# A mixture-of-experts block on one core: rewritten road to the first expert, later upper weight halves, last row group transposed behind six products

## Chip, core and metric

The kernel runs on one core of a Trainium2 chip. The metric is the device time of one execution in microseconds (us). The engines are TensorE (PE; its weight loads are listed as PEld), VectorE (DVE), ScalarE (ACT), GpSimd (POOL) and SyncE (SP). Each has its own instruction queue, and they wait for each other by semaphores only.

## What is computed

A transformer block on x of shape 2 x 2048 x 256: linear attention, then a mixture of 8 experts with 2 experts per token and a fixed capacity of 640 rows per expert. The change lies in the second half:

```python
logits = xf @ router_w.T
probs = jax.nn.softmax(logits, axis=-1)
topw, topi = jax.lax.top_k(probs, K)                       # K = 2
capacity = max(1, int(CF * N / E))                         # 640 of N = 4096 rows, E = 8
order = jnp.lexsort((-fw, fe))                             # by expert, then by falling weight
rank = jnp.arange(N * K) - starts[se]
keep = rank < capacity
disp = jnp.zeros((E, capacity + 1, D), x.dtype).at[se, pos].set(xf[st])
g = jnp.einsum('ecd,edf->ecf', disp, wg)
u = jnp.einsum('ecd,edf->ecf', disp, wu)
eo = jnp.einsum('ecf,efd->ecd', jax.nn.silu(g) * u, wd)    # D = 256, F = 1024
out = jnp.zeros_like(xf).at[st].add(contrib)
```

## The kernel before

**Stages.** All is written by hand in five queues. The attention stage walks 32 tiles of 128 tokens and writes normalised rows to the DRAM tensor `h_rows`. Then comes the road to the first expert, a chain with almost nothing beside it:

1. `choose` (L742) gives each token its two experts and weights `wgt`.
2. A search of 15 steps (L876 to L892) finds for each expert the bit pattern `cand` of the weight at the capacity limit. In each step DVE counts (`hit`, L880), PE sums the counts (L1272), and DVE picks the next pattern (L884 to L891). The 15 steps are a hardware loop of 3 turns of 5 steps.
3. `place_masks`, `place_counts`, `place_slots` (L899 to L939) turn "weight above / equal to the threshold" into a slot number for each token. They run in two parts, `PLACES = ((0, 2), (2, E))`: experts 0 and 1 first, the other six later. PE helps with four products against a triangular matrix `before` and a matrix of ones.
4. `describe(e)` (L973) splits the slot numbers of expert e into tile number (`tile_no`, `in_tile`) and row (`row_in`), makes `facts` (L962) and a one-hot matrix `onehot` (L970, four pieces), and PE's `look(e)` (L1288, 32 small products) reads off which token stands in each slot. `find_tokens` (L990) turns that into the index list `g_idx`.
5. POOL gathers the rows of expert e by five indirect DMAs of 128 rows (L496); PE transposes them (`transpose_x`, L1296) in row groups of 2, 2 and 1 tiles; ACT rounds them (`xT_h`, L634) and DVE makes the remainder (`xT_l`, L1027).

**Experts.** For each of 8 slices f of the hidden dimension, PE does `gate_up(f)` (24 products of 320 columns, 12 for each half h of the 640 rows, six for the gate and six for the up matrix), and then `down(f-1)` (15 products, L1341). ACT and DVE make `hid_h` and `hid_l` from it. In the shade of expert e the rows of expert e+1 are transposed at f = 4, 5, 6 (at 5, 6, 7 for the first expert), its weights are split into `w_h` (ACT, L625) and `w_l` (DVE, L1013), and `look(e+2)` runs at the end.

**Weights.** SP loads each expert's weights in a lower half (f 0 to 3, semaphore `raw_a`) and an upper half (f 4 to 7, `raw_b`), five DMAs and 1.5 MB each (L331). Both go into one buffer `w_raw`, so that a half is loaded as soon as the split of the expert before has read it: `expert` in the SP block (L394) waits for `sp_h` and `sp_l`.

## Time and profile before

| | |
|---|---|
| time, median of 3 runs | 678.95 us (678.22 to 679.12) |
| the profiled execution's own time | 678.13 us |
| its span in the trace | 676.0 us, 2.13 us less |
| PE busy | 568.7 us (84%) |
| DVE busy | 456.5 us (68%) |
| ACT / POOL busy | 320.0 / 269.0 us |
| chain that ended last | PE 59%, DVE 13%, issue 7% |
| mean DMA rate | 111 GB/s |

Spans and busy times come from one execution recorded by the hardware profiler. "Busy" for PE does not mean that it runs at its peak. In timeline rows the columns are start, length, engine, line, operation, output<-inputs, shapes, count, and in brackets the idle time before it with what ended it.

### The profile page before, as it was taken

The page shows a single profiled execution, that of the slowest core. Times are in us where ns is not written, and L with a number is a line of the kernel's source. Part 1 is how long each engine was busy: PE and PEld are TensorE (multiplying, and loading weights), DVE is VectorE, ACT ScalarE, POOL GpSimd, SP SyncE. Part 2 cuts the span into 40 slices and gives each one's busy share as a digit, 9 for nine tenths or more (in the row PEclk, how much of TensorE's full clock was granted, in tenths as well). Part 3 has the DMA queues.
Part 4 walks back from the last instruction along what each step waited for, and adds up shares of the span by engine and source line. Part 5 has one row for each costly group of instructions (what it writes and reads, how often), then busy time and mean ns, then how long its engine had stood idle before and what let it go on. Part 6 is the DMA issues. An engine that isn't in the chain of part 4 may idle for free.

```text
span 676.0 us, 13788 instructions
## 1 busy us (share of the span) xinstructions
PE 568.7 (84%) x4041; PEld 529.4 (78%) x4041; DVE 456.5 (68%) x1304; ACT 320.0 (47%) x717; POOL 269.0 (40%) x427
## 2 busy tenths in 40 slices
PE   4999889998997101279999999999999999999990
PEld 3577668887776000169999999999999999999990
DVE  3577889897677877867756766567667666666431
ACT  3688778886444500034534534445345444454330
POOL 5688757776678000302007025043070160442304
PEclk9999999999999555569989999999999999999996
DMA  5322268545554900144408317344174073340203
GB/s 164 94 64 78 71 194 264 189 145 162 157 190 153 264 0 0 40 133 133 133 1 213 94 44 170 95 141 102 61 198 106 18 194 95 110 102 9 32 1 39
DMA packets 91911, 75.24 MB, mean 111 GB/s; under 512 B 12108, under 2 KB 88278, under 8 KB 91864
## 3 DMA queue, kind: packets, MB, share of 16 engines
q1 hardware_dynamic: 82872, 58.77, 28.6%
q0 software_dynamic: 8992, 15.90, 11.2%
q8 instruction: 24, 0.39, 0.2%
q14 instruction: 23, 0.19, 0.1%
HBM read 52.48 MB, written 22.16 MB: 110 GB/s over the span
## 4 chain that ended last, share of the span: by engine, by line
PE 59%; DVE 13%; issue 7%; POOL 3%; ACT 2%; DMA 2%; DVEq 1%; SPq 0%; ACTq 0%; POOLq 0%
PE bank L1329 33%; PE bank L1341 15%; PE bank L1247 3%; PE bank L1292 2%; DVE hit L880 2%; PE bank L1150 2%; PE bank L1306 1%; DMA mod_all<-mod_store 1%; DVE x L847 1%; DVE st L849 1%; POOL out L506 1%; PE bank L1227 1%; PE bank L1236 1%; DMA xg<-h_rows,g_idx 1%; PE bank L1202 0%
## 5 line engine op out<-in xcount | busy, mean ns | idle before, releaser
L1329 PE MATMUL bank<-xT_h,w_h 128*128 128x320 f32 x512 | 160.2, 313 | 2.3 <-DVE xT_l L1027 1.7
L1329 PE MATMUL bank<-xT_l,w_h 128*128 128x320 f32 x512 | 159.2, 311 | 0.4 <-issue 0.4
L1329 PE MATMUL bank<-xT_h,w_l 128*128 128x320 f32 x512 | 159.0, 311 | 0.0
L496 POOL DMA_INDIRECT xg<-h_rows,g_idx x40 | 43.8, 1095 | 274.5 <-DVE g_idx L999 264.7
L1055 DVE TENSOR_TENSOR hid<-act_g,bank 128x320 f32<-128x320 f32 x128 | 62.0, 484 | 74.1 <-ACT act_g L648 59.6
L652 ACT CAST hid_h<-hid 128x320 fp32r<-128x320 f32 x128 | 58.9, 460 | 97.5 <-DVE hid L1055 92.8
L648 ACT ACTIVATE act_g<-bank 128x320 f32<-128x320 f32 x128 | 55.8, 436 | 103.3 <-PE bank L1329 96.2
L1329 PEld LDWEIGHTS bank<-xT_h,w_h 128*128 128x128 f32 x512 | 97.6, 191 | 3.0 <-DVE w_l L1013 2.1
L1329 PEld LDWEIGHTS bank<-xT_h,w_l 128*128 128x128 f32 x512 | 97.5, 190 | 0.5 <-issue 0.5
L1329 PEld LDWEIGHTS bank<-xT_l,w_h 128*128 128x128 f32 x512 | 97.5, 190 | 0.5 <-issue 0.5
L1341 PE MATMUL bank<-w_h,hid_h 128*128 128x256 f32 x320 | 91.4, 286 | 0.4 <-DVE hid_l L1060 0.4
L506 POOL DMA_INDIRECT out<-yo,s_idx x40 | 66.3, 1657 | 62.0 <-DVE yo L1045 50.7
L1060 DVE TENSOR_TENSOR hid_l<-hid,hid_h 128x320 fp32r<-128x320 f32 x128 | 62.8, 491 | 39.1 <-ACT hid_h L652 33.9
L1341 PE MATMUL bank<-w_h,hid_l 128*128 128x256 f32 x320 | 89.2, 279 | 0.0
L1341 PE MATMUL bank<-w_l,hid_h 128*128 128x256 f32 x320 | 89.0, 278 | 0.0
L1013 DVE TENSOR_TENSOR w_l<-w_raw,w_h 128x768 fp32r<-128x768 f32 x64 | 61.1, 960 | 7.9 <-ACT w_h L625 6.0
L1341 PEld LDWEIGHTS bank<-w_h,hid_h 128*128 128x128 f32 x320 | 60.2, 188 | 0.7 <-ACT hid_h L652 0.6
L1341 PEld LDWEIGHTS bank<-w_l,hid_h 128*128 128x128 f32 x320 | 60.5, 189 | 0.0
L1341 PEld LDWEIGHTS bank<-w_h,hid_l 128*128 128x128 f32 x320 | 60.3, 188 | 0.0
L1150 PE MATMUL bank<-wqkv_h,hT_h 128*128 128x256 f32 (+1 forms) x128 | 49.2, 384 | 6.0 <-DVE hT_l L819 4.7
L625 ACT CAST w_h<-w_raw 128x768 fp32r<-128x768 f32 x64 | 52.9, 833 | 0.0
L484 POOL TENSOR_TENSOR rot<-rot_a,rot_b 128x512 f32<-128x512 f32 x32 | 42.2, 1320 | 17.1 <-DVE rot_b L812 16.9
(180 smaller groups left out, 1118.2 us busy)
## 6 DMA issues: line engine op xcount, KB each, us to landing
w_raw<-wg SPq DMA_DIRECT2D x32, 256.0 KB, 3.3
w_raw<-wu SPq DMA_DIRECT2D x32, 256.0 KB, 4.4
w_raw<-wd SPq DMA_DIRECT2D x16, 512.0 KB, 6.1
x_in<-x SPq DMA_DIRECT2D x32, 128.0 KB, 2.1
q_store<-qT SPq DMA_DIRECT2D x32, 128.0 KB, 1.9
q_in<-q_store SPq DMA_DIRECT2D x32, 128.0 KB, 2.2
x_re<-x SPq DMA_DIRECT2D x32, 128.0 KB, 2.2
out<-x SPq DMA_DIRECT2D x32, 128.0 KB, 1.9
```

The lines of the kernel that those rows point to most:

```text
L484: nc.gpsimd.tensor_tensor(rot[s.par(0)][:, :], rot_a[:, :], rot_b[:, :], ALU.add).then_inc(rope_d, 1)
L496: nc.gpsimd.indirect_dma_start(out=xg[par][:, a, :], out_offset=None, in_=h2_rows, in_offset=bass.IndirectOffsetOnAxis(ap=g_idx[par][:, a: ...
L506: nc.gpsimd.indirect_dma_start(out=out_rows, out_offset=bass.IndirectOffsetOnAxis(ap=s_idx[par][:, a:a + 1], axis=0), in_=yo[:, a, :], in_ ...
L625: nc.scalar.copy(w_h[:, f, :], w_raw[:, f, :]).then_inc(sp_h, 1)
L648: nc.scalar.activation(act_g[h][:, :], bank[2 * h][:, 0:HCAP], ACT.Silu).then_inc(silu_d, 1)
L652: nc.scalar.copy(hid_h[f % 2][:, h * HCAP:(h + 1) * HCAP], hid[h][:, :]).then_inc(hh_d, 1)
L1013: V.tensor_tensor(w_l[:, f, :], w_raw[:, f, :], w_h[:, f, :].bitcast(F32), ALU.subtract).then_inc(sp_l, 1)
L1055: V.tensor_tensor(hid[h][:, :], act_g[h][:, :], bank[2 * h + 1][:, 0:HCAP], ALU.mult)\
L1060: V.tensor_tensor(hid_l[f % 2][:, h * HCAP:(h + 1) * HCAP], hid[h][:, :], hid_h[f % 2][:, h * HCAP:(h + 1) * HCAP].bitcast(F32), ALU.subtr ...
L1150: ins = MM(out, x[j][:, k, :], w[i][:, k, cols], start=n == 0, stop=n == 3 * KC - 1)
L1329: last = MM(bank[2 * h + m][:, 0:HCAP], W[i][:, f, at:at + P], XT[j][:, k, cols], start=n == 0, stop=n == 3 * KC - 1)
L1341: last = MM(bank[4 + a // 2][:, a % 2 * D:(a % 2 + 1) * D], (hid_h, hid_l)[j][f % 2][:, a * P:(a + 1) * P], (w_h, w_l)[i][:, f, 4 * P:], s ...
```

## The change

It does five things.

- The search is written out, 15 steps in a row, with no loop on DVE or PE.
- Slots are computed by a shorter formula. `before` now holds 0 above the diagonal and -1 elsewhere, so that PE delivers "rows before me minus all rows", and the running sum can be added directly. Slots are int32, tokens over the capacity just get a tile number of 5 or more, and tile numbers come from a shift by 7 bits. The first part covers expert 0 alone.
- The one-hot matrix is made in four pieces by token tile (the inner dimension) and no longer by row, and `look` waits piece by piece. `find_tokens` is one reduction.
- Row groups are (0, 1), (2,), (3, 4). The first half of the first `gate_up` waits for two groups only; the last group is transposed after its first six products, into bank 7.
- SP loads the upper weight half of expert e+1 only when the first row group of expert e+1 has been transposed (`trx_d`).

```diff
-XG = -(-CT // 2)
+ROW_GROUPS = ((0, 1), (2,), (3, 4))
+XG = len(ROW_GROUPS)
-PLACES = ((0, 2), (2, E))
+PLACES = ((0, 1), (1, E))
...
                 wait(sp, sp_h, e * FC + FC)
                 wait(sp, sp_l, e * FC + FC)
+                wait(sp, trx_d, (e + 1) * XG + 1)
                 load_weights(e + 1, FC // 2, raw_b)
...
-            nc.gpsimd.affine_select(out=before[:, :], in_=ones_b[:, :], compare_op=ALU.is_gt, fill=0.0, base=0,
+            nc.gpsimd.affine_select(out=before[:, :], in_=zeros_b[:, :], compare_op=ALU.is_gt, fill=-1.0, base=0,
                                     pattern=[[1, P]], channel_multiplier=-1).then_inc(plink_s, 1)
...
-                        .then_inc(ga_d[a // 2], 16)
+                        .then_inc(ga_d[next(g for g, t in enumerate(ROW_GROUPS) if a in t)], 16)
...
-            with dve.Fori(0, DIGITS // SEARCH) as i:
-                for j in range(SEARCH):
-                    n = i * SEARCH + j
...
+            for n in range(DIGITS):
...
-                V.tensor_scalar(need[:, lo:hi], run[:, 0, lo:hi, NT - 1], -1.0, float(CAP), ALU.mult, ALU.add)
-                for k in range(2):
-                    ins = TT(flat(pre[:, k, lo:hi, :]), flat(run[:, k, lo:hi, :]), tot[k], ALU.subtract)
-                link(ins)
-                for k in range(2):
-                    ins = TT(flat(pre[:, k, lo:hi, :]), flat(pre[:, k, lo:hi, :]), rows[k], ALU.add)
-                ins.then_inc(pre_d, 1)
+                V.tensor_scalar(above[:, lo:hi], run[:, 0, lo:hi, NT - 1], 1.0, None, ALU.add)
+                V.scalar_tensor_tensor(flat(pre[:, 0, lo:hi, :]), flat(run[:, 0, lo:hi, :]), 1.0, rel[0], ALU.add, ALU.add)
+                TT(flat(pre[:, 1, lo:hi, :]), flat(run[:, 1, lo:hi, :]), rel[1], ALU.add).then_inc(pre_d, 1)
...
-                TT(t, pre[:, 1, lo:hi, :], need_b, ALU.is_lt)
-                link(TT(at, pre[:, 1, lo:hi, :], need_b, ALU.min))
-                link(TT(t, t, mask2[:, 1, lo:hi, :], ALU.mult))
-                TT(kept, t, mask2[:, 0, lo:hi, :], ALU.add)
-                link(TT(at, at, pre[:, 0, lo:hi, :], ALU.add))
-                link(V.scalar_tensor_tensor(kept, at, float(CAP), kept, ALU.is_lt, ALU.mult))
-                link(V.scalar_tensor_tensor(at, at, 1.0, kept, ALU.add, ALU.mult))
-                link(V.tensor_scalar(at, at, -1.0, None, ALU.add))
+                link(TT(p1, p1, above_b, ALU.add))
+                TT(p0, p0, mask2[:, 0, lo:hi, :], ALU.mult)
+                link(TT(p1, p1, mask2[:, 1, lo:hi, :], ALU.mult))
+                link(V.scalar_tensor_tensor(slot[:, lo:hi, :], p0, -1.0, p1, ALU.add, ALU.add))
...
-                TT(tile_ge[:, :, :], sl.unsqueeze(2).to_broadcast([P, NT, CT + 1]),
-                   tile_thr[:, :].unsqueeze(1).to_broadcast([P, NT, CT + 1]), ALU.is_ge).then_inc(ge_d, 1)
-                dve.wait_ge(ge_d, e + 1)
-                RED(tile_no[:, :], tile_ge[:, :, 1:], AX, ALU.add).then_inc(tn_d, 1)
-                TT(in_tile[:, :, :], tile_ge[:, :, 0:CT], tile_ge[:, :, 1:], ALU.subtract).then_inc(in_d, 1)
+                V.tensor_scalar(tile_no[:, :], sl, TILE_BITS, None, ALU.arith_shift_right).then_inc(tn_d, 1)
                 dve.wait_ge(tn_d, e + 1)
+                TT(in_tile[:, :, :], tile_no[:, :].unsqueeze(2).to_broadcast([P, NT, CT]),
+                   tile_id[:, :].unsqueeze(1).to_broadcast([P, NT, CT]), ALU.is_equal).then_inc(in_d, 1)
...
-                sl = slice(part * P // 4, (part + 1) * P // 4)
-                TT(onehot[:, sl, :], iota_b[:, sl, :], row_in[:, :].unsqueeze(1).to_broadcast([P, P // 4, NT]),
+                sl = slice(part * NT // 4, (part + 1) * NT // 4)
+                TT(onehot[:, :, sl], iota_b[:, :, sl], row_in[:, sl].unsqueeze(1).to_broadcast([P, P, NT // 4]),
                    ALU.is_equal).then_inc(facts_d, 1)
...
-                V.tensor_copy(got[:, :, :], bank[7][:, 0:NV * CT].rearrange("p (v a) -> p v a", v=NV))\
-                    .then_inc(got_d, 1)
-                dve.wait_ge(got_d, e + 1)
-                lk(V.scalar_tensor_tensor(tok[:, :], got[:, 1, :], float(P), got[:, 0, :], ALU.mult, ALU.add))
-                lk(V.tensor_scalar(tok[:, :], tok[:, :], -float(P), 0.0, ALU.add, ALU.max))
-                V.tensor_copy(g_idx[par][:, :], tok[:, :]).then_inc(idx_d, 1)
+                    RED(g_idx[par][:, :], bank[7][:, 0:NV * CT].rearrange("p (v a) -> p a v", v=NV), AX, ALU.add)\
+                        .then_inc(idx_d, 1)
...
-            x_low(0, 0, 0, bk=0)
             place_slots(1)
+            x_low(0, 0, 0, bk=0)
             x_low(0, 0, 1, bk=1)
             split_low(0, 4, 4)
-            x_low(0, 0, 2, bk=2)
+            x_low(0, 0, 2, bk=7)
...
-                wait(pe, facts_d, e * 4 + 4)
                 for n in range(NT):
+                    if n % (NT // 4) == 0:
+                        wait(pe, facts_d, e * 4 + n // (NT // 4) + 1)
...
-            for g in range(XG):
+            for g in range(XG - 1):
                 transpose_x(0, 0, g, first=True)
...
-                if f == 0:
-                    wait(pe, xl_d, e * XG + XG)
                 for h in range(2):
+                    if f == 0:
+                        wait(pe, xl_d, e * XG + XG - 1 + h)
...
+                        if first and (h, m) == (0, 0):
+                            transpose_x(0, 0, XG - 1, first=True)
```

**DVE, from the counts to the tile numbers of expert 0.** Before, the eight slot operations (L932 to L939) and the four of `describe_tiles` read:

```order
L932 TENSOR_TENSOR tmp_s<-pre,need 128x64 [waits pre_d]
L933 TENSOR_TENSOR slot<-pre,need 128x64
L934 TENSOR_TENSOR tmp_s<-tmp_s,mask 128x64 [waits link_s]
L935 TENSOR_TENSOR keep<-tmp_s,mask 128x64 [waits link_s]
L936 TENSOR_TENSOR slot<-slot,pre 128x64
L937 SCALAR_TENSOR_TENSOR keep<-slot,keep 128x64 [waits link_s]
L938 SCALAR_TENSOR_TENSOR slot<-slot,keep 128x64 [waits link_s]
L939 TENSOR_SCALAR slot<-slot 128x64 [waits link_s]
L948 TENSOR_TENSOR tile_ge<-slot,tile_thr 128x192 [waits iota_d,link_s]
L951 TENSOR_REDUCE tile_no<-tile_ge 128x32 [waits ge_d]
L952 TENSOR_TENSOR in_tile<-tile_ge 128x160
L954 SCALAR_TENSOR_TENSOR row_in<-tile_no,slot 128x32 [waits tn_d]
```

Now the same stretch is:

```order
L924 TENSOR_TENSOR pre<-pre,above 128x32 [waits pre_d]
L925 TENSOR_TENSOR pre<-pre,mask 128x32 [waits link_s]
L926 TENSOR_TENSOR pre<-pre,mask 128x32
L927 SCALAR_TENSOR_TENSOR slot<-pre 128x32 [waits link_s]
L936 TENSOR_SCALAR tile_no<-slot 128x32 [waits iota_d,link_s]
L938 TENSOR_TENSOR in_tile<-tile_no,tile_id 128x160 [waits tn_d]
L940 SCALAR_TENSOR_TENSOR row_in<-tile_no,slot 128x32
```

Twelve instructions with nine waits have become seven with five, on 32 instead of 64 elements in the slot part.

**PE, from the first rows of expert 0 to its first products.** L1306 is a transposition (two for each tile and group), L1329 a product of `gate_up`. Before:

```order
L1306 MATMUL bank<-const_sb,xg 128x128 [waits ga_d0]
L1306 MATMUL bank<-const_sb,xg 128x128 x3
L1306 MATMUL bank<-const_sb,xg 128x128 [waits ga_d1]
L1306 MATMUL bank<-const_sb,xg 128x128 x3
L1306 MATMUL bank<-const_sb,xg 128x128 [waits ga_d2]
L1306 MATMUL bank<-const_sb,xg 128x128
L1329 MATMUL bank<-xT_h,w_h 128x320 [waits xl_d,sp_l]
```

Now (L1278 is the transposition, L1301 the product):

```order
L1278 MATMUL bank<-const_sb,xg 128x128 [waits ga_d0]
L1278 MATMUL bank<-const_sb,xg 128x128 x3
L1278 MATMUL bank<-const_sb,xg 128x128 [waits ga_d1]
L1278 MATMUL bank<-const_sb,xg 128x128
L1301 MATMUL bank<-xT_h,w_h 128x320 [waits xl_d,sp_l]
L1301 MATMUL bank<-xT_l,w_h 128x320
L1301 MATMUL bank<-xT_h,w_l 128x320
L1301 MATMUL bank<-xT_h,w_h 128x320
L1301 MATMUL bank<-xT_l,w_h 128x320
L1301 MATMUL bank<-xT_h,w_l 128x320
L1278 MATMUL bank<-const_sb,xg 128x128 [waits ga_d2]
L1278 MATMUL bank<-const_sb,xg 128x128 x3
```

The last group, now two tiles and four transpositions, stands behind six products, and the six products wait for two groups only.

**SP, head of the loop over experts.** L331 (now L327) loads the upper half of the next expert. Before:

```order
L405 UNCONDITIONAL_BRANCH
L405 ISA
L331 ISA [waits sp_l,sp_h]
L331 DMA w_raw<-wg 128x4x128
L331 ISA
L331 DMA w_raw<-wg 128x4x128
L331 DMA w_raw<-wu 128x4x128 x2
L331 ISA
L331 DMA w_raw<-wd 128x4x256
```

Now:

```order
L402 UNCONDITIONAL_BRANCH
L402 ISA
L75 ISA [waits sp_l,sp_h]
L327 ISA [waits trx_d]
L327 DMA w_raw<-wg 128x4x128
L327 ISA
L327 DMA w_raw<-wg 128x4x128
L327 DMA w_raw<-wu 128x4x128 x2
L327 ISA
L327 DMA w_raw<-wd 128x4x256
```

A wait for `trx_d` stands ahead of the first of the five DMAs; the load of the lower half of the expert after it follows in the same queue.

## Rows read from the trace of the kernel before

**Rows 1.** Stretch, length; busy PE, PEld, DVE, ACT, POOL; clock, DMA share, GB/s

```profile
298.20:339.90 41.70, 41.23 (x325) 40.92 (x323) 31.56 (x68) 20.56 (x42) 5.21 (x5) 1.00 0.38 113
```

**Rows 2.** Timeline of DVE, steps of the search (the first count of each step)

```profile
232.68 0.48 DVE L880 TENSOR_SCALAR_CACHE_REDUCE hit<-valT,cand 128x256 bf16<-128x256 f32 x1 [0.22 <-DVE valT L875]
...
234.92 0.48 DVE L880 TENSOR_SCALAR_CACHE_REDUCE hit<-valT,cand 128x256 bf16<-128x256 f32 x1
...
241.65 0.48 DVE L880 TENSOR_SCALAR_CACHE_REDUCE hit<-valT,cand 128x256 bf16<-128x256 f32 x1
...
244.38 0.48 DVE L880 TENSOR_SCALAR_CACHE_REDUCE hit<-valT,cand 128x256 bf16<-128x256 f32 x1 [0.52 <-DVE cand L891]
...
267.48 0.23 DVE L894 TENSOR_SCALAR thr_sel<-const_sb,cand 128x8 f32<-128x8 f32 x1 [0.21 <-DVE cand L891]
```

**Rows 3.** Timeline of DVE from the masks to the index list of expert 0

```profile
268.61 0.73 DVE L904 TENSOR_TENSOR mask<-wgt,thr_b 128x64 bf16<-128x64 f32 x2
...
270.32 0.17 DVE L918 TENSOR_SCALAR need<-run 128x2 f32<-128x2 f32 x1
...
271.16 0.23 DVE L932 TENSOR_TENSOR tmp_s<-pre,need 128x64 f32<-128x64 f32 x1
...
272.96 0.36 DVE L948 TENSOR_TENSOR tile_ge<-slot,tile_thr 128x192 f32<-128x192 f32 x1
...
273.94 0.56 DVE L962 TENSOR_TENSOR facts<-vals,in_tile 128x160 bf16<-128x160 bf16 x2
274.42 2.49 DVE L970 TENSOR_TENSOR onehot<-iota_b,row_in 128x1024 bf16<-128x1024 bf16 x4
279.11 0.17 DVE L994 COPY got<-bank 128x10 f32<-128x10 f32 x1 [2.21 <-PE bank L1292]
...
279.72 0.17 DVE L999 CAST g_idx<-tok 128x5 int32<-128x5 f32 x1
279.80 1.85 DVE L904 TENSOR_TENSOR mask<-wgt,thr_b 128x192 bf16<-128x192 f32 x2
```

**Rows 4.** Timeline of PE, the look of expert 0

```profile
276.96 2.11 PE L1292 MATMUL bank<-facts,onehot 128*128 128x10 bf16 x32 [7.17 <-DVE onehot L970]
```

**Rows 5.** Timeline of POOL, gathers of row tiles 2 and 3 of expert 0

```profile
284.44 1.41 POOL L496 DMA_INDIRECT xg<-h_rows,g_idx  x1 [0.30 <-issue]
286.15 0.94 POOL L496 DMA_INDIRECT xg<-h_rows,g_idx  x1 [0.30 <-issue]
```

**Rows 6.** Timeline of PE, second and last row group, first product of expert 0

```profile
289.68 1.11 PE L1306 MATMUL bank<-const_sb,xg 128*128 128x128 f32 x4 [2.13 <-DMA xg<-h_rows,g_idx]
291.22 0.69 PE L1306 MATMUL bank<-const_sb,xg 128*128 128x128 f32 x2 [0.43 <-DMA xg<-h_rows,g_idx]
293.64 0.60 PE L1329 MATMUL bank<-xT_h,w_h 128*128 128x320 f32 x1 [1.72 <-DVE xT_l L1027]
```

**Rows 7.** Timeline of DVE, remainder of the first row group

```profile
288.21 0.69 DVE L1027 TENSOR_TENSOR xT_l<-bank,xT_h 128x512 fp32r<-128x512 f32 x1 [0.89 <-ACT xT_h L634]
```

**Rows 8.** Busy time in chosen stretches, from the first product on

```profile
293.64:298.20 4.56, 4.56 (x17) 4.56 (x18) 0.52 (x2) 0.44 (x2) 0.00 (x0) 0.50 0.96 280
...
339.90:346.10 6.20, 6.20 (x50) 6.20 (x51) 1.45 (x2) 0.53 (x3) 0.00 (x0) 0.72 0.01 3
...
359.52:364.23 4.71, 3.97 (x27) 3.62 (x26) 1.94 (x3) 1.72 (x4) 4.07 (x3) 1.00 0.91 292
```

**Rows 9.** Chain that ended last: start, length, what; 24 undisturbed products

```profile
366.00 3.52 PE bank L1329 x24
```

**Rows 10.** Timeline of SP, first loads of a lower weight half

```profile
330.02 0.93 SPq L331 DMA_DIRECT2D w_raw<-wg  x2
```

**Rows 11.** Busy time in a stretch at the end of those loads

```profile
338.00:340.00 2.00, 1.53 (x15) 1.34 (x14) 1.31 (x3) 1.46 (x3) 0.00 (x0) 1.00 0.00 0
```

**Rows 12.** Timeline of ACT, first split of an upper half, then the next silu

```profile
333.68 0.84 ACT L625 CAST w_h<-w_raw 128x768 fp32r<-128x768 f32 x1
335.77 0.44 ACT L648 ACTIVATE act_g<-bank 128x320 f32<-128x320 f32 x1 [1.25 <-PE bank L1329]
```

More of the change, by code:

```diff
@@ L1268, in _ @@
             last.then_inc(r_pe, 1)
[L1269 to L1272 removed]
+            for n in range(DIGITS):
+                pe.wait_ge(cnt_d, n + 1)
+                MM(bank[1][:, 0:3], same_e[:, :], cnt[:, :], start=True, stop=True).then_inc(tot_d, 1)
             pe.wait_ge(r_dve, 3)
```

91 lines of the change are left out of this document (38 added, 53 removed).

## The prediction

> **What bounds the kernel now.** I read the busy time by stretch first, then the timelines of the stretch in which PE is idle. From 298.2 to 339.9 us PE is busy 41.23 of 41.70 us at full clock [rows 1], and the stretches after it look alike: in the experts the bound is PE, and what other engines save there is worth nothing. Ahead of them stands the road. From the first count of the search at 232.68 us [rows 2] to the first product of expert 0 at 293.64 us [rows 6] there are 61 us in which each step waits for the one before it, mostly on DVE. A microsecond saved on that chain is a microsecond of the kernel, until the rows of expert 0 are gathered. After that three transpositions, ACT and DVE stand between the last gather and the first product.
>
> **The search, written out.** The first counts of two neighbouring steps stand 2.24 us apart; across the turn of the loop it is 241.65 to 244.38, 2.73 us [rows 2]. So a turn costs 0.49 us. Two turns give 0.98 us. The idle time before the first step is 0.22 us and before `thr_sel` 0.21 us, where waits elsewhere on the road leave 0.03 us: 0.19 and 0.18 us more. Sum: 1.35 us. The bound below is nothing, if straight code is fetched too slowly; the attention stage is partly straight code too, and no row there shows it, so I take 1.35. The Trainium skill (Advanced Engine Details and Errata, Control Flow Timing) gives about 108 ns for a compare-and-branch. Two turns would then be an estimated 0.22 us, and this trace doesn't agree: its turn takes 0.49 us.
>
> **Masks, counts, slots, tiles.** Two masks take 0.73 us at 64 elements and 1.85 us at 192 [rows 3], 4.4 ns an element, so 0.45 us at 32: 0.3 saved. From `need` at 270.32 to `tmp_s` at 271.16 are 0.84 us for two subtractions, a wait and two additions; now one small operation and two additions without a wait between them, about 0.42; with shorter scans ahead of them (an estimated 0.1) the saving is 0.5. Slots: 271.16 to 272.96, 1.80 us for eight operations of which each waited one costs some 0.23. Now three waited ones and one that overlaps, 0.76: 1.05 saved. Tiles: 272.96 to 273.94, 0.98 us; now a shift (about 0.2) and a comparison of 160 elements (0.36 at 192), 0.56: 0.4 saved.
>
> **The look.** The one-hot matrix takes 2.49 us in four pieces, and PE begins at 276.96 when all are there and is read at 279.11 [rows 3, 4]: 2.15 us. Now PE works behind each piece. A quarter of the look (about 0.5 us) is shorter than a piece (0.62), so after the last piece only a quarter and the pipe remain, 0.65 us: 1.5 saved. The open cost is the one-hot itself: its inner run shrinks from 32 to 8 elements. No row shows such a pattern. Below, it costs nothing (0.62 us a piece); above, it falls to the rate of the remainder operation, 0.69 us for 512 elements [rows 7], that is about 1.3 us a piece and 2.8 us in all. It is nearest to today's row (same types, same count, still neighbours in memory), so I take nothing. The Trainium skill (VectorE: DVE Perf Modes, What auto-detection actually checks) has 16-bit tensors with step 1 run two elements a cycle, which also speaks for no change; the trace's 0.62 us for 1024 elements agrees for the long run only.
>
> **Tokens.** 279.11 to 279.89 (279.72 + 0.17) becomes one operation of some 0.17 [rows 3]: 0.6 saved.
>
> Up to the index list: 1.35 + 0.3 + 0.5 + 1.05 + 0.4 + 1.5 + 0.6 = **5.7 us**.
>
> **The first products.** I keep the clock of the old trace, counted from the index list. POOL's issue for tile 3 ends at 287.09 and its rows free PE at 289.68, 2.6 us later; tile 2's issue ends at 285.85 [rows 5], so its rows are there by 288.45. Then the transposition of one tile (0.69 [rows 6]), ACT (0.4) and DVE (0.4, both estimates, half of 0.69 and a hand-over) and 0.15: first product at 290.2 in place of 293.64. DVE could be later than that, because `place_slots(1)` now stands ahead of the first remainder (288.21 before [rows 7]). Before, DVE was free at 287.32, 0.89 us ahead of that remainder. Masks of seven experts add 0.3, scans 0.15, the four slot operations 1.55, and the counts give back 0.4 (estimates from the rows above, scaled to 224 elements): 288.9, and with two remainders (0.69 and 0.4) 290.0. So it just fits. The start gains 3.4 us. The last group is landed at 291.2 [rows 6] and PE comes to it after six products at 0.27 us, at 291.9: no wait. Its four transpositions (1.1 us) now lie inside the products. But at half clock the product rate is half too: 17 products in 4.56 us at 0.50 [rows 8], so if the clock rises as long after the start as before, they displace about four products which run later at full clock, 24 in 3.52 us [rows 9]: 0.6 us. Net **2.8 us**. ACT's table load now follows the last rounding and ends about 0.4 us after the first half is ready; PE has the second half to do meanwhile.
>
> **Upper weight halves.** In expert 1 one `gate_up` takes 4.71 us, with gathers, scatters and the upper half of expert 2 at 292 GB/s beside it [rows 8], and 3.52 us undisturbed [rows 9]. PE waits there for no semaphore. The load goes to a time after most of the scatters: **1.0 us** of the 1.19, since its new place has some traffic as well. Does it come late? Five such DMAs are issued from 330.02 on and no byte moves after 338.0 [rows 10, 11], 8 us at most. In expert 0 the first group of expert 1 is transposed at f = 5, one slice before that of f = 6. A slice is an estimated 5.7 us: 24 products 3.52 [rows 9], the 15 of `down` at 256 columns by the same rate 1.76, transpositions 0.4 to 0.5. ACT rounds the f = 6 group just before 333.68, so the one of f = 5 is transposed at about 326.5, and the half is there at 334.5 at the latest. ACT wants it at 333.68 and has until 335.77 [rows 12] for 0.84 us of work: no delay of PE. In later experts it is issued at f = 4 and wanted at f = 6, some 13 us later. Behind it in SP's queue stands only the next lower half, wanted 15 us on.
>
> **Sum.** 5.7 + 2.8 + 1.0 = 9.5 us. The profiled execution took 678.13 us, so 668.6; it lies 0.8 below the median of the runs, so I predict **669.4 us** as a median.
>
> **Rivals.**
> - *The dip of the clock after expert 0 disappears.* From 339.9 to 346.1 the granted clock is 0.72 on average [rows 8]: PE does a look there, with its 10-column products, and then runs for a while at 1.2 in place of 2.4 GHz; (1 - 0.72) of 6.2 us is 1.7 us. The last remainder ahead of this look now has two tiles, not one, and everything is shifted in time. If the clock holds, 667.7 us. 0.15.
> - *The one-hot in short runs goes at the slow rate.* Plus 2.8: 672.2 us. 0.10.
> - *The early start is eaten.* DVE's longer queue ahead of the first remainder, or the last rows landing late while PE stands before them in order. The 2.8 us are lost, and the traffic stall only moves to another place: 673.2 us. 0.10.
> - *Upper halves come late, slower than before.* ACT would wait in `split_high` at f = 6 in seven experts, behind it the next silu. To turn 9.5 us of gain into over 1.4 us of loss each would have to cost 1.6 us, so with 13 us of cover and about 3 us that PE can spare, a load would have to take 17 us or more; it takes 8. 0.03: about 681.
> - *The road is shorter but the kernel isn't*, because gathers wait for stores into `h_rows`: these were issued long before. 0.02: 678.
>
> **How the numbers follow.** My forecast has 0.60. A measurement of this kernel tells 0.2% (1.4 us) from no change. Faster by more than that: 0.60 + 0.15 + 0.10 + 0.10 = 0.95. The range goes from 665.8 (clock dip gone and 2 us more on the road, where most terms are estimates) to 673.2, which takes in the slow one-hot and the eaten start.
>
> **What the profile would show.** Steps of the search 2.24 us apart throughout; 5.7 us less from its first count to POOL's first gather; one-hot pieces of 0.6 us (1.3 if the rival holds); PE's transpositions of the last group after six products with no DMA wait ahead; first product some 9.1 us earlier than at 293.64; all `gate_up` of expert 1 at 3.5 us; ACT's `w_h` of f = 4 never waiting long on DMA. The prediction fails if PE waits anew between 285 and 300 us, or in every expert at f = 6.

## The result

Median of before 679.12 us (678.22 to 681.04), of the changed kernel **673.86 us** (671.94 to 675.32), five runs each: a ratio of 0.9922, 95% interval 0.9902 to 0.9942. The gain is 5.3 us; forecast were 9.5 us, and the time lies 0.7 us above the range. Both sides of the balance were off: the road gained more than forecast, and the experts behind it gave some 6 us back. (In the two profiles the spans differ by only 2.9 us, 676.0 to 673.1, because in the changed kernel's the search also happens to start 1.4 us later, at 234.09 in place of 232.68.)

**The road.** DVE in the changed kernel, two neighbouring steps of the search, its end, and the way to the index list (answers to [rows 2, 3]):

```profile
234.09 0.48 DVE L876 TENSOR_SCALAR_CACHE_REDUCE hit<-valT,cand 128x256 bf16<-128x256 f32 x1
...
236.24 0.48 DVE L876 TENSOR_SCALAR_CACHE_REDUCE hit<-valT,cand 128x256 bf16<-128x256 f32 x1
...
266.39 0.23 DVE L890 TENSOR_SCALAR thr_sel<-const_sb,cand 128x8 f32<-128x8 f32 x1
...
270.80 2.49 DVE L956 TENSOR_TENSOR onehot<-iota_b,row_in 128x1024 bf16<-128x1024 bf16 x4
274.00 0.17 DVE L970 TENSOR_REDUCE g_idx<-bank 128x5 int32<-128x10 f32 x1 [0.72 <-PE bank L1264]
```

Steps are 2.15 us apart, not 2.24, and from the first count to `thr_sel` it is 32.30 us in place of 34.80. The one-hot in runs of 8 costs what it did in runs of 32: 2.49 us. The index list stands 39.91 us after the first count, before 47.04.

PE in the changed kernel, the first products (answers to [rows 4, 6]):

```profile
271.54 2.43 PE L1264 MATMUL bank<-facts,onehot 128*128 128x10 bf16 x32 [3.36 <-DVE onehot L956]
...
282.71 0.69 PE L1278 MATMUL bank<-const_sb,xg 128*128 128x128 f32 x2 [0.48 <-DMA xg<-h_rows,g_idx]
284.41 0.61 PE L1301 MATMUL bank<-xT_h,w_h 128*128 128x320 f32 x1 [1.01 <-DVE xT_l L999]
...
286.15 1.05 PE L1278 MATMUL bank<-const_sb,xg 128*128 128x128 f32 x4
```

The look starts behind the first one-hot piece; the last group is transposed after six products with no DMA wait ahead of it. From the first count to the first product: 60.96 us before, 50.32 now, a gain of 10.6 us (forecast 9.1).

**What was given back.** From the first product to the end of the span it was 676.0 - 293.64 = 382.4 us; it is 673.1 - 284.41 = 388.7. By the looks these 6.3 us fall apart as follows: expert 0, from its first product to the look at its end, takes 47.7 us in place of 46.3; expert 1, to the next look, 46.7 in place of 48.1; the next four experts together 186.8 in place of 182.1; the rest 107.5 in place of 105.9. The forecast had 0.6 us more for expert 0 (the transpositions that now stand behind its first product), 1.0 us less for expert 1, and nothing for the others. So experts 0 and 1 together cost nothing more, and the whole loss is in the experts after them.

The first place at which something changed is expert 0. SP in the changed kernel, the loads of the upper weight half of expert 1 and behind them the first of the next lower half (answers to [rows 10]):

```profile
317.97 0.95 SPq L327 DMA_DIRECT2D w_raw<-wg  x2
319.01 1.77 SPq L327 DMA_DIRECT2D w_raw<-wu  x2
320.98 0.37 SPq L327 DMA_DIRECT2D w_raw<-wd  x1
321.68 1.21 SPq L327 DMA_DIRECT2D w_raw<-wg  x2
```

ACT in the changed kernel, the split that waits for that half (answers to [rows 12]):

```profile
324.46 0.37 ACT L632 CAST xT_h<-bank 128x256 fp32r<-128x256 f32 x1
326.69 0.83 ACT L623 CAST w_h<-w_raw 128x768 fp32r<-128x768 f32 x1 [1.86 <-DMA w_raw<-wd]
```

PE in the changed kernel, the look behind it:

```profile
332.09 2.04 PE L1264 MATMUL bank<-facts,onehot 128*128 128x10 bf16 x32 [1.31 <-DVE xT_l L999]
```

The half is issued at 317.97, and the lower half of expert 2 starts right behind it at 321.68. Its last part lands at 326.7, 8.7 us after the first issue; ACT stood for it for 1.86 us. Behind ACT's split stand two silus and the last rounding, behind these the last remainder on DVE, behind it the look: PE is idle 1.31 us (0.47 before). TensorE's clock behind this look is the same in both profiles. Busy time in the 8.95 us from the look on (columns as in [rows 1]: the granted clock is the third figure from the end), in the changed kernel:

```profile
332.09:341.04 8.95, 8.95 (x74) 8.95 (x75) 2.72 (x6) 1.34 (x3) 0.00 (x0) 0.81 0.01 2
```

In the kernel before:

```profile
339.90:348.85 8.95, 8.95 (x72) 8.95 (x73) 2.37 (x5) 1.42 (x4) 0.00 (x0) 0.81 0.01 2
```

The second place is every later expert. Their looks are 46.7 us apart on average (four intervals from 378.80 to 565.63), before 45.5 (387.97 to 570.08). PE in the changed kernel, the last product of f = 2 in expert 3:

```profile
441.67 0.31 PE L1301 MATMUL bank<-xT_h,w_l 128*128 128x320 f32 x1
```

ACT in the changed kernel, the silus around it:

```profile
440.25 0.44 ACT L646 ACTIVATE act_g<-bank 128x320 f32<-128x320 f32 x1 [0.94 <-PE bank L1301]
444.74 0.44 ACT L646 ACTIVATE act_g<-bank 128x320 f32<-128x320 f32 x1 [2.96 <-remote]
449.20 0.44 ACT L646 ACTIVATE act_g<-bank 128x320 f32<-128x320 f32 x1 [2.26 <-PE bank L1301]
```

The last product of f = 2 starts at 441.67 and is over by 442.0. ACT has nothing else to do, and its silu starts at 444.74. PE's signal came 2.7 us late: the profile has an update of the semaphore that ACT waits for just before 444.74, but no instruction that ended then, and calls that "remote". So it is the signal that is late, and not ACT that stands. The next one came late too (449.20; its products were done at 445.5), and PE then waited for `hid`. The kernel before shows the second of these, not the first, and had enough time to spare that it cost little, some 0.2 us an expert (45.5 us, against 45.3 in e17 below, the same kernel without a late signal).

POOL in the changed kernel, the first gather and the first scatter beside these silus:

```profile
437.63 1.02 POOL L494 DMA_INDIRECT xg<-h_rows,g_idx  x1 [31.31 <-DVE g_idx L970]
...
444.04 1.62 POOL L504 DMA_INDIRECT out<-yo,s_idx  x1 [0.30 <-issue]
```

The late signal was due 4.3 us after the first gather began, and 2 us before the first scatter stands in the trace.

### The profile page after: what moved, and what is told of

Its sections match the earlier page's. It is cut to its first block, busy times and chain, and to the rows that moved or that the text cites. A ratio compares the mean times of both kernels' runs of the same rounds, so it can differ in the third digit from the quotient of the medians.

```text
span 673.1 us, 13689 instructions
## 1 busy us (share of the span) xinstructions
PE 575.1 (85%) x4041; PEld 533.3 (79%) x4041; DVE 448.5 (67%) x1260; ACT 320.1 (48%) x717; POOL 263.6 (39%) x428
## 4 chain that ended last, share of the span: by engine, by line
PE 61%; DVE 12%; issue 5%; POOL 3%; DMA 2%; ACT 2%; another core or an unknown queue 1%; SPq 1%; DVEq 0%; ACTq 0%; POOLq 0%
PE bank L1301 33%; PE bank L1315 14%; DVE hit L876 3%; PE bank L1219 3%; PE bank L1122 2%; PE bank L1264 2%; PE bank L1278 1%; DVE x L845 1%; PE bank L1199 1%; DVE st L847 1%; DMA w_raw<-wd 1%; POOL out L504 1%; PE bank L1208 1%; DMA x_in<-x 1%
## 5 line engine op out<-in xcount | busy, mean ns | idle before, releaser
L1301 PE MATMUL bank<-xT_h,w_h 128*128 128x320 f32 x512 | 160.8, 314 | 4.6 <-DVE hid L1027 2.8
L1301 PE MATMUL bank<-xT_l,w_h 128*128 128x320 f32 x512 | 158.7, 310 | 0.0
L1301 PE MATMUL bank<-xT_h,w_l 128*128 128x320 f32 x512 | 158.7, 310 | 0.0
L494 POOL DMA_INDIRECT xg<-h_rows,g_idx x40 | 40.8, 1020 | 270.1 <-DVE g_idx L970 260.3
L1301 PEld LDWEIGHTS bank<-xT_h,w_h 128*128 128x128 f32 x512 | 97.4, 190 | 6.9 <-issue 4.9
L1301 PEld LDWEIGHTS bank<-xT_l,w_h 128*128 128x128 f32 x512 | 97.3, 190 | 0.1
L1301 PEld LDWEIGHTS bank<-xT_h,w_l 128*128 128x128 f32 x512 | 97.0, 189 | 0.0
L504 POOL DMA_INDIRECT out<-yo,s_idx x40 | 63.8, 1596 | 66.8 <-DVE yo L1017 55.5
L623 ACT CAST w_h<-w_raw 128x768 fp32r<-128x768 f32 x64 | 52.9, 834 | 1.9 <-DMA w_raw<-wd 1.9
```

The costliest lines, as they stand in the source:

```text
L494: nc.gpsimd.indirect_dma_start(out=xg[par][:, a, :], out_offset=None, in_=h2_rows, in_offset=bass.IndirectOffsetOnAxis(ap=g_idx[par][:, a: ...
L504: nc.gpsimd.indirect_dma_start(out=out_rows, out_offset=bass.IndirectOffsetOnAxis(ap=s_idx[par][:, a:a + 1], axis=0), in_=yo[:, a, :], in_ ...
L623: nc.scalar.copy(w_h[:, f, :], w_raw[:, f, :]).then_inc(sp_h, 1)
L1301: last = MM(bank[2 * h + m][:, 0:HCAP], W[i][:, f, at:at + P], XT[j][:, k, cols], start=n == 0, stop=n == 3 * KC - 1)
```

## The experiments

The experiments came to stand on four chips, which I number 2 to 5; the chip of the result above I count as chip 1, though the record doesn't name it. The kernel before, run beside each, took 679.1 us on chip 1, 681.5 on 2, 681.1 on 3, 675.7 on 4 and 674.7 to 675.4 on 5. This turned out to be part of the answer. Each chip was used in one stretch of time, so "chip" below can't be told apart from the hour. Each median is over 4 to 12 executions, 5 for the changed kernel on chip 1. "Road" is from the first count to the first product, "expert" the mean of the four intervals between looks from the end of expert 1 on.

| run | chip | median us | ratio (95%) | road | expert |
|---|---|---|---|---|---|
| changed kernel | 1 | 673.86 | 0.9922 (0.9902 to 0.9942) | 50.3 | 46.7 |
| e1_load_early | 2 | 679.38 | 0.9968 (0.9949 to 0.9987) | 50.4 | 47.4 |
| e2_before_load_late | 2 | 679.64 | 0.9972 (0.9955 to 0.9989) | 61.2 | 45.5 |
| e3_search_looped | 2 | 678.97 | 0.9962 (0.9945 to 0.9979) | 52.9 | 46.8 |
| e4_before_unrolled | 2 | 677.87 | 0.9955 (0.9936 to 0.9974) | 58.7 | 46.3 |
| e5_changed_again | 3 | 677.82 | 0.9953 (0.9940 to 0.9966) | 50.3 | 47.1 |
| e6_gather_later | 3 | 680.26 | 0.9989 (0.9967 to 1.0011) | 50.4 | 46.8 |
| e7_scatter_later | 3 | 666.89 | 0.9801 (0.9787 to 0.9815) | 50.4 | 45.4 |
| e8_before_one_op | 3 | 687.51 | 1.0102 (1.0078 to 1.0126) | 60.6 | 47.7 |
| e9_scatter_first | 4 | 670.63 | 0.9931 (0.9907 to 0.9955) | 50.3 | 46.0 |
| e10_before_scatter_later | 4 | 674.90 | 0.9994 (0.9981 to 1.0007) | 61.2 | 45.2 |
| e11_scatter_later_load_early | 4 | 665.88 | 0.9864 (0.9846 to 0.9881) | 50.5 | 45.3 |
| e12_scatter_same_time | 4 | 667.40 | 0.9876 (0.9859 to 0.9893) | 50.4 | 45.3 |
| e13_wait_long_true | 5 | 667.13 | 0.9877 (0.9853 to 0.9900) | 50.5 | 45.3 |
| e14_wait_for_dve | 5 | 668.01 | 0.9888 (0.9865 to 0.9911) | 50.4 | 45.4 |
| e15_changed_third | 5 | 668.31 | 0.9896 (0.9874 to 0.9919) | 50.4 | 45.4 |
| e16_wait_and_load_early | 5 | 666.23 | 0.9870 (0.9847 to 0.9893) | 50.4 | 45.4 |
| e17_before_itself | 5 | 675.49 | 0.9997 (0.9984 to 1.0009) | 61.2 | 45.3 |
| e18_scatter_same_time_again | 5 | 666.91 | 0.9874 (0.9851 to 0.9897) | 50.4 | 45.4 |

### The late load and the search, each undone and each alone (chip 2)

e1 takes this line out of the changed kernel, e2 adds it to the kernel before:

```diff
+                wait(sp, trx_d, (e + 1) * XG + 1)
                 load_weights(e + 1, FC // 2, raw_b)
```

e3 puts the loop of the search back in the changed kernel, e4 writes it out in the kernel before:

```diff
-            with dve.Fori(0, DIGITS // SEARCH) as i:
-                for j in range(SEARCH):
+            for n in range(DIGITS):
...
-            with pe.Fori(0, DIGITS // SEARCH) as i:
-                for j in range(SEARCH):
+            for n in range(DIGITS):
```

> The changed kernel, with only the moved upper weight halves put back to where they were (SP no longer waits for the transposition of the next rows). Theory A, the moved load is what ate the gain: after the first product the changed kernel took 388.7 us against 382.4, and the load stands in both of the places I found (in expert 0 ACT waited 1.9 us for it, with a late remainder, a late look and the low clock behind that; in each later expert PE lost some 1.3 us more between look and f = 4, where the load used to run). Then this version is about 6 us faster than the changed kernel: ratio to the kernel before about 0.984, 668 us, looks of later experts 45.5 us apart, no DMA wait of ACT near 326. Theory B, the loss per expert comes from something else that changed (other row groups, the look, code): only expert 0's part comes back (2 us) and the stall in expert 1 returns (1 us): ratio 0.990 or above, looks still 46.8 us apart.

> The kernel before, with only the moved upper weight halves added (one wait of SP). Theory A: slower than before by the same 5 to 6 us, ratio about 1.008, looks 46.8 us apart. Theory B: no more than the 1 us gain in expert 1 against some loss in expert 0: ratio 0.998 to 1.003, looks 45.5 us apart.

> The changed kernel with the search of 15 steps as a loop of 3 turns again, everything else as changed. By the steps of the two traces (34.80 against 32.30 us from the first count to thr_sel) writing it out gave 2.5 us, so this version is 2.5 us slower than the changed kernel, ratio to before about 0.996. Rival: the longer straight code costs something later (code to be brought in for DVE and PE, other places of the loops in memory): then the back end is shorter by some us and the ratio is near 0.992 or below.

> The kernel before with only the search written out. By the two traces 2.5 us faster: ratio 0.9963. My own prediction's sum has 1.35 us for it: 0.9980. Rival as in the run before: 1.0 or above if the longer code costs later what it gives in the search.

My theory fell. With the load put back, the experts take 47.4 us, not 45.5: the silu of f = 2, second half, comes 20.7 us after the look (19.2 in e3 with the load late, 16.4 where it should be). So the moved load doesn't make PE's signals late; on this chip it went with a smaller lateness. And with the load late in the kernel before, nothing is lost per expert, and the kernel is 0.28% faster, 1.9 us, an interval that leaves out 1. In the changed kernel the late load was worth more on this chip: e1 stands at 0.9968 and e3 at 0.9962 although e3's search is 2.5 us longer, which makes some 2.9 us.

These runs also test the price that the prediction gave the late load. It was read from one product stage of expert 1, f = 3, 4.71 us in place of 3.52 [rows 8]. The same stage in e2, where the half is issued 11.8 us after the start of the stage:

```profile
360.23:365.44 5.21, 4.28 (x26) 3.64 (x25) 1.47 (x3) 1.20 (x2) 4.30 (x4) 1.00 0.67 143
```

And in e17, the kernel before on chip 5, with the half loaded at its old time (issued from 357.69 on):

```profile
360.51:364.02 3.51, 3.51 (x26) 3.51 (x25) 2.26 (x5) 1.55 (x3) 2.90 (x3) 1.00 0.85 276
```

With the load moved away the stage stayed long; with the load beside it, on chip 5, the stage was short.

The search written out is worth 2.5 us in every run: from the first count to `thr_sel` 34.8 us in e2, e3, e8, e10, e17 and 32.3 us in all others. As a whole e4 gains 0.45%, or 3.1 us. Its experts take 46.3 us in the profile, though no edit stands behind the search; a signal of f = 3 comes 0.7 us later than in the kernel before on chip 1. Whether that is the edit or the chip isn't known, since the kernel before wasn't profiled on chip 2. The medians there leave e4 a gain no smaller than what its search saved, which speaks for the chip.

### When gathers and scatters are issued (chip 3)

e6 puts a clearing of a spare tile ahead of the gathers; e7 holds the scatters back; e8 gives the kernel before the index list in one operation (and the multiplied tile numbers that it needs):

```diff
+                wait_apart(pool, pz, e, apart)
+                nc.gpsimd.memset(idle_p[:, :], 0.0).then_inc(pz, 1)   # e6 alone
                 gather(e + 1, 1 - par)
+                wait_apart(pool, trx_d, (e + 1) * XG + 1, apart)      # e7 alone
                 scatter(e - 1, 1 - par)
```

> The changed kernel itself once more, on the chip of the next three runs, so that these have something to stand against. All theories: 0.992, looks of the experts 46.8 us apart.

> The changed kernel, with a clearing of a spare tile on POOL (some 0.6 us) ahead of the gathers in the loop of experts 1 to 6. What is found so far: in every expert, some 4.5 us after POOL's first gather, PE's signals to ACT come late by 2 to 4 us; PE does not stop by itself, but it has only about 1.5 us to spare until it needs what follows. In the kernel before the gathers start 12.6 us after the look and one signal is caught (that of f = 3, first half); in the changed kernel they start at 12.0 us and the signal ahead of it (f = 2, second half) is caught too. Theory P, phase: the shorter way from the look to the index list moved the gathers 0.6 us forward and into this signal. Then this version puts them back and the experts take 45.5 to 46 us: 5 to 8 us faster than the changed kernel, ratio about 0.983. Rival Q: the stall comes from something else that changed (the waits in the look, the row groups, the length of the code) and not from the time of the gathers: then the experts still take 46.8 us, ratio 0.992.

> The changed kernel, with POOL's scatters of the loop held back until the first group of the next rows is transposed (f = 4), some 9 us later than now. Theory G, the gathers alone make PE's signals late: the stall stays where it is (silu of f = 2, second half, 19.1 us after the look) at least at its start, and the time with it: ratio 0.99 or a little under, or above if scatters meet the weight loads. Theory S, the scatters (whose first starts 18.4 us after the look, shortly before the late signals come) make them late: the experts take 45.4 us up to there and any new stall stands 9 us later; ratio 0.983.

> The kernel before, with only the index list made by one operation instead of four, so that the gathers start 0.6 us earlier in every expert (and on the road to the first). Theory P, phase: the signal of f = 2, second half, is now caught here too, the experts take 46.5 us or more instead of 45.5, and the version is slower than before by 5 us: 1.008. Rival Q: only the 0.6 us on the road: 0.999, experts 45.5 us.

e6 didn't do what it was made for. POOL in e6, in expert 3:

```profile
441.38 0.53 POOL L525 MEMSET idle_p<- 128x512 f32 x1 [30.87 <-DVE g_idx L975]
442.14 1.03 POOL L496 DMA_INDIRECT xg<-h_rows,g_idx  x1 [0.23 <-issue]
```

The first gather of an expert starts about 1 us after the index list anyway (440.96 on DVE here), and the clearing fits into that time: the gathers moved by 0.1 us. It says nothing on the phase, and its higher time comes with more time at low clock in expert 1 (granted clock 0.61 from 331.35 to 340.00 and again 0.83 from 352 to 362 us).

e8 is the test of the phase (the time of the gathers within an expert) that worked. Its gathers start 12.0 us after the look (12.6 before), the silu of f = 2, second half, comes at 20.7 instead of 16.4 (the latter on chips 1 and 2), and saving 0.6 us on the road made the kernel 1.0% slower.

e7 is the other end. ACT in e5 in expert 4, the silus of f = 2 and of f = 3, first half:

```profile
484.80 0.44 ACT L646 ACTIVATE act_g<-bank 128x320 f32<-128x320 f32 x1 [0.93 <-PE bank L1301]
489.38 0.44 ACT L646 ACTIVATE act_g<-bank 128x320 f32<-128x320 f32 x1 [3.06 <-remote]
493.90 0.44 ACT L646 ACTIVATE act_g<-bank 128x320 f32<-128x320 f32 x1 [2.34 <-PE bank L1301]
```

The same three silus in e7:

```profile
482.49 0.44 ACT L647 ACTIVATE act_g<-bank 128x320 f32<-128x320 f32 x1 [0.94 <-PE bank L1302]
484.25 0.44 ACT L647 ACTIVATE act_g<-bank 128x320 f32<-128x320 f32 x1 [0.23 <-PE bank L1302]
487.78 0.44 ACT L647 ACTIVATE act_g<-bank 128x320 f32<-128x320 f32 x1 [1.33 <-PE bank L1302]
```

In e7 each silu follows its products at once, also at f = 4 to 6 where the scatters now are, beside the weight loads. The same chip, the same minutes, one wait of POOL: 677.82 to 666.89 us. With the lateness gone the gain over the kernel before is 14.2 us by medians, more than the 9.5 forecast, since the kernel before has late signals to lose as well.

e7 does two things at once: it moves the scatters by some 10 us, and it makes POOL wait between gathers and scatters. Which of the two cures isn't shown. That the signal of f = 2 was due before the first scatter stands in the trace (441.98 against 444.04 in the changed kernel) speaks against the plain reading that a scatter under way holds it up.

### Order, place, and waits (chips 4 and 5)

e9 swaps the two calls. e10 holds the scatters back in the kernel before, e11 is e7 without SP's wait. e12 to e14 put one wait between gathers and scatters that moves neither; e16 is e12 without SP's wait; e15 and e17 are the two kernels unchanged, e18 is e12 again:

```diff
                 gather(e + 1, 1 - par)
+                wait_apart(pool, gu_d, e * 2 * FC + 5, apart)    # e12, e16, e18
+                wait_apart(pool, idx_d, e + 2, apart)            # e13
+                wait_apart(pool, hid_d, e * 2 * FC + 5, apart)   # e14
                 scatter(e - 1, 1 - par)
```

> The changed kernel, with the scatters of the last rows ahead of the gathers of the next in POOL's loop, back to back as now. Holding the scatters back to f = 4 took away every late signal of PE (experts 45.4 us, kernel 0.980). Theory O, order: late signals come when scatters are issued right behind gathers whose rows are still on their way; with the order turned round they are small or gone, experts 45.3 to 45.8 us, ratio 0.981 to 0.984. Theory R, run: ten such DMAs back to back make them late in either order: experts 46.5 us or more, ratio 0.990 or above. The gathers then begin 21.5 us after the look and their first group is wanted at 27: if that is too late, PE waits there for rows, which the trace would show as a DMA wait ahead of the transpositions.

> The kernel before, with only the scatters of the loop held back until the first group of the next rows is transposed. Before, one signal came late by 2.3 us and cost PE next to nothing (0.1 us an expert). If the late signals are what the scatters cost, this gives 0.1 to 0.2 us in each of six experts, 1 us in all, and 1 us in expert 1, where a product stage stood at 4.71: ratio 0.997. If scatters next to weight loads cost anything by themselves, 1.0 or above.

> The changed kernel with the scatters held back, but with the upper weight halves where they were before (SP doesn't wait for the transposition). This isolates what the late load is worth when no signal comes late. If its only good was that it took traffic from the time of gathers and scatters, it is worth nothing now, and in expert 0 it costs (ACT waited 1.9 us for the half there): this version is 0.5 to 1.5 us faster than the one with scatters held back, ratio 0.978 to 0.980. If the load at f = 2 slows gathers or PE's signals even without scatters: experts over 45.4 us, ratio 0.983.

> The changed kernel with a wait of POOL between gathers and scatters that is over before the gathers are all issued (first product half of f = 2), so that the scatters start at the same time as now. A control: the late signal of f = 2, second half, is due 2 us before the first scatter stands in the trace. If it is the time of the scatters, nothing changes: experts 47 us, ratio 0.995. If POOL without a wait runs ahead of what the trace shows, and it is the waiting as such that helped, the signal of f = 2 comes in time (silu 16.4 us after the look in place of 19.1) and the ratio is 0.985 to 0.99.

e12 had its silu in time and experts of 45.3 us. I took that for a cure by a mere wait, and made three runs to find out which kind of wait:

> The changed kernel with a wait of POOL between gathers and scatters for something that has been true since before the gathers (the index list), so that POOL is never held, but the same instructions stand there as in the run that waited for the first half of f = 2. Theory N, an instruction in between is enough: silu of f = 2, second half, 16.4 us after the look, experts 45.3 us, about 8 us faster than the changed kernel. Theory H, POOL's queue has to be held: everything as in the changed kernel, silu at 19.1 us, experts 47 us.

> The same, with POOL waiting for DVE's product of f = 2, first half, which comes some 1 us after PE's signal that was waited for before. Theory H, held by whom doesn't matter: experts 45.3 us. Theory E, it is the wait for a signal of PE that brings PE's signals out in time: experts 47 us, silu at 19.1 us.

> The changed kernel again, on the chip of these runs. Experts 47 us, ratio 0.992 to 0.996.

> The changed kernel with the wait for PE's first half of f = 2 between gathers and scatters, and without the late load of the upper weight halves. With scatters held back to f = 4 the early load was 0.0012 of the kernel faster than the late one stood on another chip. Here traffic of gathers, scatters and weights falls together again at f = 2 to 4. If only PE's late signals made that dear: experts 45.3 us, expert 0 0.7 us shorter, ratio 0.001 to 0.002 under that of the late load. If the traffic itself is dear: experts 46 us or more.

The control e15 undid it. The changed kernel itself, with no wait of POOL, has no late signal on this chip: experts 45.4 us, 668.3 us in all. So e13 and e14 stood where there was nothing to cure, and e12 most likely too: the changed kernel wasn't run on chip 4, but the kernel before took there what it takes on chip 5 (675.7 and 674.7 to 675.4 us).

> The kernel before, unchanged, for its profile on this chip. If signals of PE come late here: before at 679 to 682 us, silu of f = 3, first half, 22.3 us after the look. If not: 674 to 676 us, that silu at 19.8 us, experts 45.2 us (as the version with scatters held back had them). The ratio should be 1.000 within 0.002.

> The changed kernel with POOL's wait between gathers and scatters that moves neither, once more. On a chip with late signals: if the wait does nothing, experts 47 us and a ratio of 0.992 to 0.996; if it cures them, experts 45.4 us and 0.980. On a chip without them it tells nothing new: 45.4 us, 0.988.

e17 agrees: the kernel before on chip 5 has its silu of f = 3, first half, at 19.9 us after the look, on chip 1 at 22.3. e18 stood on chip 5 again, so whether such a wait does anything where signals are late isn't known. e9 gains less than e12 on its chip, 0.9931 against 0.9876: its gathers start 22.1 us after the look, and the rows come too late for the first transposition: from the start of the products ahead of it to the transposition it is 4.24 us in place of 3.52, and PE waited for DMA in five experts, 0.25 to 0.59 us each, 2.35 us in all. e10 (0.9994) shows that holding the scatters back is worth nothing in the kernel before on chip 4.

Chip 5 has both kernels without late signals, and shows the late load without them. ACT in e15 (late load), the split of expert 0 that waits:

```profile
325.66 0.83 ACT L623 CAST w_h<-w_raw 128x768 fp32r<-128x768 f32 x1 [2.32 <-DMA w_raw<-wd]
```

PE in e15, the look behind it:

```profile
331.05 2.10 PE L1264 MATMUL bank<-facts,onehot 128*128 128x10 bf16 x31 [1.77 <-DVE xT_l L999]
```

The same split on ACT in e16 (early load):

```profile
322.20 0.84 ACT L623 CAST w_h<-w_raw 128x768 fp32r<-128x768 f32 x1
```

The same look on PE in e16:

```profile
328.81 2.20 PE L1264 MATMUL bank<-facts,onehot 128*128 128x10 bf16 x32 [0.55 <-DVE xT_l L999]
```

And busy time in the 8.95 us from that look on, in e15:

```profile
331.05:340.00 8.95, 8.95 (x62) 8.95 (x63) 1.44 (x2) 1.30 (x3) 0.00 (x0) 0.62 0.01 2
```

In e16:

```profile
328.81:337.76 8.95, 8.95 (x82) 8.95 (x83) 3.81 (x9) 2.01 (x5) 0.00 (x0) 1.00 0.01 2
```

In e17, the kernel before:

```profile
341.32:350.27 8.95, 8.95 (x73) 8.95 (x74) 2.51 (x5) 1.43 (x4) 0.00 (x0) 0.81 0.01 2
```

The late load delays the look (PE idle 1.77 us in place of 0.55). In this pair of profiles the clock behind the look differs too: it falls to 0.62 on average in e15, with 62 matmul records in the stretch, and not at all in e16, with 82. Expert 0 from its first product to this look: 48.4 us in e15, 46.8 in e16, 46.0 before. From this look to the next: 47.9, 45.3, 46.5. By these profiles the late load costs 4.4 us.

But these two profiles are the ends of the range. In the twenty profiles of this study PE idles 0.47 to 0.55 us ahead of this look with the early load, and the granted clock in the 8.95 us from it is 0.81 five times and 1.00 three times. With the late load PE idles 0.76 us in e2 and 1.16 to 2.32 us in the versions of the changed kernel, and the clock is 0.81 five times, the changed kernel on chips 1 and 3 among them, and 0.62 seven times. So the late load goes with a lower clock, but the idle time alone doesn't decide it: e13 idles 1.99 us and has 0.81, e7 idles 1.50 us and has 0.62.

By medians e15 and e16 are 2.1 us apart, and e12 and e11 on chip 4 1.5 us, with overlapping intervals; and each of these pairs differs by a second edit, POOL's wait. The pair that differs by the late load alone is e18 and e16, 0.9874 and 0.9870: 0.3 us. What the late load costs where no signal is late isn't shown beyond the idle time of PE; it lies between nothing and some 2 us.

## Why the prediction was wrong

The step that failed is the one that gave the experts a fixed time: "in the experts the bound is PE, and what other engines save there is worth nothing". The sum had nothing for them; the profile has 6.3 us, all of it behind expert 1. The term for the upper weight halves failed as well, in its cause. Term by term:

**Up to the index list, 5.7 us.** Right in kind, too small: 7.1 us (47.04 to 39.91). The search is the term: 1.35 us forecast, 2.5 measured. I priced the turns and the waits around the loop, and took the step of 2.24 us for granted. But a step written out takes 2.15 us: DVE's idle time ahead of `beats` fell from 0.30 to 0.21 us. The Trainium skill (Advanced Engine Details and Errata, Control Flow Timing) gives about 108 ns for a compare-and-branch. The loop here cost far more than its branches by that figure: 2.5 us over two turns and 15 steps. The other terms give 4.6 us together for 4.35 forecast.

**First products, 3.4 us earlier from the index list on.** Right: 3.5 (10.64 - 7.13). DVE reached the first remainder in time, and "no wait" ahead of the last group came out.

**Upper weight halves, "1.0 us" gained and "no delay of PE".** The reasons of this step failed, and its size on chip 1 came out by luck. The price came from the stage of 4.71 us, which I put down to the traffic of the half beside it. In e17 the same stage takes 3.51 us with 276 GB/s beside it, in e2 it takes 5.21 with the half moved away. Such long stages of expert 1 stand in profiles with late signals (before, e1, e2, e4, e8, 4.7 to 6.0 us) and in none of those from chip 5. ACT in the kernel before, the silus at the start and at the end of the long stage:

```profile
359.60 0.44 ACT L648 ACTIVATE act_g<-bank 128x320 f32<-128x320 f32 x1 [2.04 <-remote]
...
364.15 0.44 ACT L648 ACTIVATE act_g<-bank 128x320 f32<-128x320 f32 x1 [2.35 <-remote]
```

Both came late, with the mark "remote". So the sign of what limited the changed kernel was already in the trace that I forecast from. What stops PE within the stage, where it waits for no semaphore, isn't shown. As to the delay, my times were nearly right (issue 8.7 us before the last byte, where I had "8 us at most"; ACT wanted the half at 324.8), but I gave ACT until the next silu and didn't follow the chain behind it: split, silu, rounding of the last group, remainder, look. There PE was idle 0.8 us longer, and expert 0 took 1.4 us more where 0.6 was forecast for other causes. That behind the half "stands only the next lower half" was true; whether that half slowed the one awaited isn't shown. The net of this step hung on the chip: on chip 1 expert 1 gave 1.4 us back, so that 0.8 lost and 1.4 gained stand near the 1.0 forecast; on chip 2 the late load alone gained 1.9 us in the kernel before (e2, whose profile doesn't show where); on chip 5 it gained nothing and cost up to 2 us. The rival "upper halves come late" had the right mechanism for one expert of seven, and asked for seven.

**What the sum didn't have.** It treated the experts as 45.5 us each, whatever stands ahead of them. The edits to the look and the index list also run in each expert, and issue its gathers 0.6 us earlier; they moved a transfer. On chips 1, 2 and 3 PE's signals come late behind the gathers, and the shift brought one more of them into that time, at 1.2 to 1.7 us an expert (46.7 against 45.5 on chip 1; 47.1 on chip 3, against 45.4 in e7). e8 shows that making the index list sooner is enough for it, and e7 that it doesn't happen when POOL waits and the scatters are held back. On chip 5 it doesn't happen at all; there the changed kernel took 668.3 us and gained 6.4, and its variants with a wait of POOL up to 8.5. So on that chip, too, the forecast of 9.5 was 1 to 3 us too high, although the road alone gave 10.7 there (61.15 to 50.42). Experts 0 and 1 took 3.9 us more in e15's profile than in e17's; the late load is the candidate for that, at the unsettled price above.

**Rivals.** The one-hot at the slow rate: refuted (2.49 us). The eaten start: refuted. The clock dip gone: it wasn't in the profile that was forecast (0.81 in both kernels), and with the late load it was deeper in seven of twelve profiles (0.62). Of the signs of failure that the forecast named, a new wait of PE in every expert came true, but at f = 3 and 4 and not at f = 6.

**What stays open.** Why PE's signals come late on chips 1 to 3 and not on chip 5 (nor, most likely, on chip 4), and by what path gathers and scatters delay them. It isn't loading of code. The DMA queues of the changed kernel on chip 1, from 440 to 530 us, where each of two experts lost its 1.3 us:

```profile
## 3 DMA queue, kind: packets, MB, share of 16 engines
q1 hardware_dynamic: 10560, 6.29, 23.1%
q0 software_dynamic: 2213, 3.86, 22.9%
```

No instruction packet moved there; over the whole run 24 and 23 did, on queues q8 and q14.

## What to carry to other kernels

A saving on an engine that isn't the bound still moves what that engine triggers: follow the moved transfer to what it now meets, in every turn of the loop and not only at its start. When a load is put later, follow the one who waits for it to the end of its chain. When one stage is longer than its neighbours and a transfer stands beside it, look at what the other engines waited for there before the transfer gets the blame. When two variants are compared, take two that differ by one edit. Before a cure is believed, run the sick kernel beside it on the same chip: here the control removed a finding. What to take from this study is the changed kernel with scatters held back: with the late load it gave 0.9801 on a chip with late signals (e7), without it 0.9864 on one without (e11). Neither was run on the other kind of chip.

## What was not expected of the hardware

- PE's signals reached ACT up to 4.3 us after the last product they stood for (2.7 us in the changed kernel, 4.3 in e1), on chips 1 to 3, some 4 to 12 us after POOL's first gather of ten indirect DMAs back to back; PE itself went on meanwhile, with pauses of 0.3 to 1.2 us in some stages of expert 1 that no semaphore explains.
- 276 GB/s beside a product stage left it at 3.51 us (e17).
- The same kernel differed by chip: the kernel before 674.7 to 681.5 us, the changed one 668.3 to 677.8 us.
- A loop of three turns with its register-valued waits cost 2.5 us against 15 steps written out.
- An operation on POOL of 0.53 us ahead of an indirect DMA moved it by only 0.1 us.
